# Scores of source tile 7 made by ScalarE and GpSimd in place of VectorE's pass, in the last layer of a graph network on one core

## The reference, cut to what matters

```python
for h in range(Ws.shape[0]):
    Wx = x @ Ws[h] + Wb[h]
    d = Wx.shape[-1]
    s = Wx[v_tgt] @ a_w[h, :d] + Wx[v_src] @ a_w[h, d:] + a_b[h]
    s = jax.nn.leaky_relu(s, negative_slope=0.2)
    alpha = _segment_softmax(s, v_tgt, n)
    outs.append(jax.ops.segment_sum(alpha[:, None] * Wx[v_src], v_tgt, num_segments=n))
```

## Time and profile before

| | |
|---|---|
| time, median of 3 runs | 2313.96 us (2309.75 to 2316.66) |
| profiled execution, own time | 2314.35 us |
| its span, first to last instruction | 2312.5 us |
| mean granted TensorE clock | 0.96 |
| PE busy | 2082.5 us, 90% |
| DVE busy | 1573.0 us, 68% |
| ACT busy | 955.7 us, 41% |
| POOL busy | 656.9 us, 28% |
| the 80 steps of the last layer | 2008.6 to 2276 us, 34.0 us for each of heads 1 to 5 |

### The profile page before, as it was taken

The page is one execution under the profiler, slowest core; times in us unless marked ns, Lnnn a source line. Parts: engine busy times, 40 slices in busy tenths (PEclk is TensorE's granted clock), DMA queues, the critical chain, the costliest instruction groups (busy, mean ns, idle before and its releaser), DMA issues. The chain is left out here.

```text
span 2312.5 us, 39812 instructions
## 1 busy us (share of the span) xinstructions
PE 2082.5 (90%) x15006; PEld 1625.6 (70%) x15006; DVE 1573.0 (68%) x3095; ACT 955.7 (41%) x1446; POOL 656.9 (28%) x488
## 2 busy tenths in 40 slices
PE   5999979899899999899999899999798996888883
PEld 5999947788788888788888788888685553333331
DVE  6779754778664778664778664778755035899974
ACT  0222213666333666333666333666330032144452
POOL 0000015300554200553200454200340000278883
PEclk8999989999999999999999899999999997999997
DMA  2000042789711688711788711688965100000001
GB/s 74 24 24 35 24 143 63 130 142 150 156 44 53 126 146 147 158 47 50 128 144 146 159 40 57 116 147 144 187 145 122 37 9 22 0 1 1 1 0 45
DMA packets 488367, 195.82 MB, mean 85 GB/s; under 512 B 441289, under 2 KB 457673, under 8 KB 488181
## 3 DMA queue, kind: packets, MB, share of 16 engines
q1 hardware_dynamic: 488181, 193.31, 41.2%
HBM read 62.94 MB, written 25.45 MB: 38 GB/s over the span
## 5 line engine op out<-in xcount | busy, mean ns | idle before, releaser
L718 PE MATMUL psum<-turned_probability_parts,values_high 125*128 125x125 bf16 x1600 | 281.8, 222 | 57.8 <-DMA turned_probability_parts<-probability_parts 28.7
L919 DVE CUSTOM_DVE_ANT_0 probabilities<-psum,counts 125x1250 f32<-125x1250 f32 x160 | 233.6, 1460 | 125.8 <-PE psum L720 125.3
L1467 ACT ACTIVATE probabilities<-probabilities,row_peaks 125x1250 f32<-125x1250 f32 x160 | 214.4, 1340 | 182.2 <-DVE row_peaks L923 182.2
L720 PE MATMUL psum<-turned_probability_parts,values_low 125*128 125x125 bf16 x1600 | 281.4, 222 | 0.0
L719 PE MATMUL psum<-turned_probability_parts,values_high 125*128 125x125 bf16 x1600 | 280.9, 221 | 0.0
L1667 DVE SCALAR_TENSOR_TENSOR probability_parts<-probabilities,row_masses,probability_parts 125x1250 bf16<-125x1250 f32 x160 | 248.4, 1553 | 20.2 <-ACT probability_parts L1479 18.5
L2004 POOL TENSOR_TENSOR logs_and_shifts<-logs_by_source,target_shifts_spread 125x1250 f32<-125x1250 f32 x80 | 208.1, 2618 | 106.4 <-ACT target_shifts_spread L2139 65.2
L1479 ACT ACTIVATE probability_parts<-probabilities,row_masses 125x1250 bf16<-125x1250 f32 x160 | 214.0, 1338 | 48.0 <-DVE row_masses L931 34.6
L718 PEld LDWEIGHTS psum<-turned_probability_parts,values_high 125*128 125x128 bf16 x1600 | 159.0, 99 | 81.4 <-issue 73.9
L2245 PE MATMUL psum<-probabilities_turned,values_and_ones 125*65 125x512 f32 (+1 forms) x480 | 192.5, 546 | 22.8 <-ACT probabilities_turned L2156 12.4
L703 ACT ACTIVATE norm_std<-norm_moments,norm_eps 125x1 f32<-125x1 f32 x120 | 35.2, 294 | 314.0 <-DVE norm_moments L699 313.9
(11 more groups left out here) (327 smaller groups left out, 5061.9 us busy)
## 6 DMA issues: line engine op xcount, KB each, us to landing
weight_stage<-in_L_gnn_m_w SPq DMA_DIRECT2D x32, 256.0 KB, 2.8
block_inputs_kept<-nodes SPq DMA_DIRECT2D x8, 896.0 KB
counts_kept<-counts_by_target_rows SPq DMA_DIRECT2D x10, 625.0 KB, 3.2
logs_kept<-counts SPq DMA_DIRECT2D x1, 5468.8 KB
nodes<-block_inputs_kept SPq DMA_DIRECT2D x12, 448.0 KB
turned_probability_parts<-probability_parts SPq DMA_TRANSPOSE x320, 3.6
counts_by_target<-counts_kept SPq DMA_DIRECT2D x2, 2187.5 KB
logs_by_source<-logs_kept SPq DMA_DIRECT2D x1, 4375.0 KB
```

The lines of the kernel that those rows point to most:

```text
L718: pe.matmul(out, lh, rh, start=first, stop=False, skip_group_check=True)
L720: return pe.matmul(out, ll, rh, start=False, stop=last, skip_group_check=True)
L919: dve.tensor_tensor_reduce(prob[0:TILE, T % 2, :], scores, fx.count_src[0:TILE, i, 0:NODES], scale, MASKED, ALU.add, ALU.max, p[:, 0:1]).t ...
L1467: nc.scalar.activation(prob[0:TILE, T % 2, :], prob[0:TILE, T % 2, :], ACT.Exp, bias=fx.peak[0:TILE, T % 2, 1:2], accum_out=fx.mass[0:TILE ...
```

## The change

In tile 7 of each head VectorE makes no score. ScalarE does it in two parts with GpSimd: it reads the spread target scores from PSUM, adds the source score (`lift`, scaled as the rest is) and takes the positive part (Relu), into `prob`. GpSimd then adds the offset into the same buffer, behind its offset 8. Since max(t, −s) + s = max(t + s, 0), the exponential of this tile takes 0.2 s as its bias (`calm`) in place of s. Two small tables are made at the start of the layer by VectorE. All counts of waits are adapted: score 8 also waits for the Relu, offset 9 for the add, exp 7 for the add.

```diff
+        lift = place("source_lifts", [128, HEADS3], F32)
+        calm = place("source_fifths", [128, HEADS3], F32)
...
+        LIFT = 7
+        def lifts(T):
+            return (T + TILES - 1 - LIFT) // TILES
+        def scores(T):
+            return T - lifts(T)
...
-                if T >= 2:
-                    pool.wait_ge(scored, T - 1)
+                if T >= 2 and (T - 2) % TILES == LIFT:
+                    pool.wait_ge(lifts_added, lifts(T - 1))
+                elif T >= 2:
+                    pool.wait_ge(scored, scores(T - 1))
                 nc.gpsimd.tensor_tensor(offset[0:TILE, T % 2, :], lw.logs[0:TILE, j, :], shifts[0:TILE, h % 2, :],
                                         ALU.add).then_inc(offset_ready, 1)
+                if j == LIFT + 1:
+                    n = lifts(T)
+                    pool.wait_ge(lifted, n)
+                    pool.wait_ge(offset_ready, T)
+                    at = prob[0:TILE, (T - 1) % 4, :]
+                    nc.gpsimd.tensor_tensor(at, at, offset[0:TILE, (T - 1) % 2, :], ALU.add).then_inc(lifts_added, 1)
...
+            dve.tensor_scalar(lift[0:TILE], column[0:TILE, LIFT, HEADS3:WAYS], BEND3, None, ALU.mult).then_inc(cols_ready, 1)
+            dve.tensor_scalar(calm[0:TILE], column[0:TILE, LIFT, HEADS3:WAYS], 0.2, None, ALU.mult).then_inc(cols_ready, 1)
...
-                dve.scalar_tensor_tensor(prob[0:TILE, T % 4, :], region(3)[0:TILE], bend[0:TILE, j, h:h + 1],
-                                         offset[0:TILE, T % 2, :], ALU.max, ALU.add).then_inc(scored, 1)
+                if j != LIFT:
...
+                    if j == LIFT + 1:
+                        dve.wait_ge(lifted, lifts(T))
+                    dve.scalar_tensor_tensor(prob[0:TILE, T % 4, :], region(3)[0:TILE], bend[0:TILE, j, h:h + 1],
+                                             offset[0:TILE, T % 2, :], ALU.max, ALU.add).then_inc(scored, 1)
...
+            def lifted_scores(T):
+                h = T // TILES
+                act.wait_ge(scored, scores(T))
+                act.wait_ge(pv, T - 3)
+                nc.scalar.activation(prob[0:TILE, T % 4, :], region(3)[0:TILE], ACT.Relu, bias=lift[0:TILE, h:h + 1]).then_inc(lifted, 1)
...
-                act.wait_ge(scored, T + 1)
+                if j == LIFT - 1:
+                    lifted_scores(T + 1)
+                if j == LIFT:
+                    act.wait_ge(lifts_added, lifts(T + 1))
+                    source = calm[0:TILE, h:h + 1]
+                else:
+                    act.wait_ge(scored, scores(T + 1))
+                    source = column[0:TILE, j, HEADS3 + h:HEADS3 + h + 1]
                 nc.scalar.activation(prob[0:TILE, T % 4, :], prob[0:TILE, T % 4, :], ACT.Exp,
-                                     bias=column[0:TILE, j, HEADS3 + h:HEADS3 + h + 1], scale=1.0 / UNIT3).then_inc(exped, 1)
+                                     bias=source, scale=1.0 / UNIT3).then_inc(exped, 1)
```

## The result

The changed kernel takes 2319.9 us (median of 19 runs, 2310.7 to 2324.0) where the kernel before takes 2313.9 (median of 19, 2309.1 to 2318.1). The ratio is 1.0020 with a 95% interval of 1.0013 to 1.0028: slower by 4.6 us (3.0 to 6.5). The profiled execution took 2320.4 us, its span is 2318.5 and its mean granted clock 0.959, so it may stand beside the execution of before (2314.35, span 2312.5, 0.96).

The account below looks back on a forecast made before the run. VectorE was the bound by shares, but around score 7 the chain of waits ran through TensorE. Terms 0.3 + 0 + 0.25 + 0 + 2.8 + 1.6 = 4.95 us gave 2319.3, 2318.9 as median; range 2312.5 to 2322.5.

Parts of the forecast that it names:

- Score 7 removed, heads 1 to 5: VectorE before step 7's peaks: its wait for L2199 grows from 0.84 to 2.3 us, gain 0; bounds 0 and 7.2 us.
- Is anything later in those heads: Heads 1 to 5: Relu 1.34 and GpSimd's add 2.80 us stay hidden, cost 0 with 0.2 us to spare.
- Head 0: First head: the add delays weigh 7 past weigh 8's old start, +0.25 us net; bounds −0.65 and +0.8.
- Head 7: Last head: uncovered add costs 2.80 us, TensorE's lower clock after 4.8 us of idleness costs 1.6 (one slow weigh).
- Start of the layer: Two small VectorE operations on a 125x8 tile cost 0.3 us; bounds 0 and 0.4.
- Rival 1: TensorE's clock doesn't fall in the last head: 3.35 us more instead of 4.95, 2317.3 us; chance 0.20.
- Rival 2: VectorE's saving arrives, at most six heads x 1.43 = 8.6 us, giving 2310.3 us; chance 0.08.
- its help from the clock: Heads 1 to 6: slow weigh 3 granted full clock, 9 us in all, for a time below 2307; half of 0.08.
- Rival 3: GpSimd's add holds up every head: at 3.37 us, 7.85 us more, 2321.8; chance 0.15 shared with rival 4.
- rival 4: ScalarE's Relu doesn't fit, exp 6 comes late; needs 1.9 us more than reckoned; chance 0.15 shared with Rival 3.

## Why the prediction was right, and what in it was not

The forecast of 2318.9 us, 4.95 more than before, stands against 2319.9 measured and 4.6 (3.0 to 6.5) by the ratio. It came right by its mechanism: nothing gained in heads 1 to 5, and the loss in head 7 from the uncovered add and the clock behind it.

**Score 7 removed, heads 1 to 5: cost 0.** Right. The wait for the spreading was forecast at 2.3 us and is 2.28 in heads 2 to 5; heads 2 to 6 are unchanged; without head 7 the ratio is 0.9994. The kernels with no score 7 exclude that GpSimd's add had eaten a gain. But the 0.84 us of air hang on a condition that I had not seen: weigh 3 is slow. Where a head ran at full clock, VectorE had no air at all behind score 7 (head 1 of the kernel with the tables alone); such a head takes 33.05 us with score 7, 32.39 without it, and 32.85 with it lifted (head 1 of the changed kernel). So at full clock a missing score is worth 0.66 us, and the longer way over ScalarE and GpSimd gives 0.46 of it back. The step is right for the clock that heads 2 to 5 get, and 0.2 us per head wrong at the other.

**Is anything later in those heads.** Right, closely: the add was taken at 2.80 us and takes 2.83, the Relu at 1.34 and takes 1.30. Weigh 7 of head 4 runs straight into weigh 8, which does not come later. The Trainium skill's ratio ("GPSIMD Engine Reference", section 3.1) would have given 2.97; the trace, 2.83 to 1.52, says 1.86 for this pair, of which the faster also reads PSUM.

**Head 0: +0.25.** Borne out, though not from the pair of traces alone, where it is −0.74. From the first score to the first copy, the traces fall into groups: 34.89 to 34.97 (seven traces) and 35.84 to 35.96 (two) without the lift, 35.20 to 35.22 (two) and 36.10 to 36.17 (two) with it. Lifted and not lifted are about 0.25 us apart; the 1 us between the groups of one kind is in the first weighs of the head (three in 9.06 us before, in 8.02 after), which some traces have slow and others not, with the same instructions up to there. They are the traces that had the quick start of the layer, so part of those 2.5 us comes back here. My working had a slip: its parts add up to 2039.4 for the end of exp 7, not 2039.6; the trace has weigh 7 begin at 2039.67 (2041.31, less the 2.68 of the later start, plus the 1.04 of the faster weighs), so the written figure was the better one.

**Head 7: 2.80 for the add, 1.6 for the clock.** Right: 4.32 us for the 4.4 forecast, the add 2.9 of it and the clock 1.4. The gap itself was 3.7 us and not 4.8: I had let weigh 76 end at 2267.36, as before, but exp 76 now stands behind the Relu of step 77, so weigh 76 is later by 1.2 us (its own wait for exp 76 is 1.37 instead of 0.19). The price of the slow weigh fits in part by luck. The 3.79 us of the earlier trace rows were no weigh at the lower level alone: in its 3.96 us by the timeline the granted clock was 0.62 and then 0.53, and a weigh wholly at 0.50 takes 4.43 us (head 4 without score 7). In head 7 too the clock came back before long, 0.78, 0.50 and 0.87 over six microseconds, so the mixed price held. The slow turning back behind the head, 0.55 us, was not in the sum, and is not clearly the change's.

**Start of the layer: +0.3.** Too high: some 0.1 to 0.2 us between traces with the same clock there, and nothing that the times could tell.

**The rivals.** Rival 1 (the clock stays up) is refuted by the stretch of 0.50, and the kernel with a filled gap shows what it would have given. The row that spoke for it, a gap of 1.98 us in front of full clock at the start of head 7, holds for the kernel before and not for others: behind the same gap the two weighs took 6.08 us instead of 4.39 without score 7, with tile 8 and with GpSimd's pass twice. Rival 2 is refuted by heads 0 to 6 alone and by both runs without score 7; its help from the clock is what the kernel with tile 4 got. Rival 3 and rival 4 do not occur at the measured durations, and doubling GpSimd's pass shows that rival 3's mechanism is there, just beyond them. Where my reasons failed is in the experiments, and mostly by the clock: 1.7 us per head in one kernel, some 5 us in one head of two others, a slow weigh that stayed when its gap was filled. The other two misses, tile 8 and tile 4, were waits behind GpSimd's add that I had left out or taken as too short.

## What to carry to other kernels

Before work is taken from the busiest engine, look at what it does right behind that place: if it waits there for another engine, the wait will grow by what is saved. Ask instead which of its results the chain picks up, and take the work out in front of that; then read the queues that the relief passes through, since one instruction behind a long wait can give it all back. Where a slower engine does a pass instead, the steady state may hide it and the last round will not; a gap that it opens on TensorE is to be priced with the clock behind it.

## What the hardware showed beyond that

- **A slow weigh that its gap does not explain.** Weigh 3 of heads 2 to 5 takes 3.87 to 3.96 us in the kernel before, in head 4 at a clock of 0.62 and 0.53, and it takes 3.89 to 3.96 with the gap in front cut from 1.79 to 0.39 us. In heads that follow each other at 32.0 us it takes 2.27 in every one. With tile 8 (heads of 34.02 and 34.47 us) it also takes 2.27 in all six, though the gap is 1.78 or 1.79 (2.21 in head 6), and with score 7 twice (heads of 34.60 us, gap of 1.78) it took 2.27 in heads 1 to 3. The end of the longer gap in head 7 is otherwise: filled from 3.69 to 0.75 us, it kept the clock. A gap alone is no measure of whether the clock will fall.
- **A long low stretch that belongs to the kernel.** Without score 7, head 4 ran at about 0.50 for some 13 us, for 4.9 us of time, in both of two profiled executions; with score 7 twice, a head of 38.81 us appeared too. A difference of 0.05 us per head went before it. What sets it is not settled, and so a change that should cost nothing can cost 0.2%.
- **Two lengths for one GpSimd pass.** 125x1250 adds take 2.40 or 2.84 us by which of the buffers they use: the longer where the halves of the two double buffers have the same parity. The same pass doubled, offset 7, took 2.83 in heads 1, 3 and 5 and 2.39 in heads 2 and 4; the in-place add, odd buffers only, 2.83.
